# Turned source rows kept in SBUF replace one gather of 32 in the second stage of a graph network kernel

## What is computed

```python
h = relu(layernorm(x))
msg = relu(cat(h[src], h[dst], edge_attr) @ msg_W1 + b1) @ msg_W2 + b2
agg = segment_sum(msg, dst)
x = x + layer_norm(h + relu(cat(h, agg) @ upd_W1 + c1) @ upd_W2 + c2)      # layer 0
h = relu(layernorm(x))
x_l, x_r = h @ W_l.T + b_l, h @ W_r.T + b_r                                # 4 heads of 32
z = leaky_relu(x_l[src] + x_r[dst], 0.2)        # every node also has a loop to itself
alpha = softmax over the edges of a target of (z . att)
x = x + elu(segment_sum(alpha * x_l[src], dst) + bias)                     # layer 1
```

## Time and profile before

| | |
|---|---|
| median of 3 runs | 4952.78 us (4950.47 to 4958.61) |
| the profiled execution | 4911.11 us, span 4909.3 us |
| instructions | 83259 |
| busy share | PE 71%, PEld 56%, DVE 47%, ACT 43%, POOL 60% |
| mean granted TensorE clock | 0.784 of 2.4 GHz |
| indirect gathers | 1517 in stage one, 1553 in stage two |
| stage one, stage two | about 77 to 2445 us and 2472 to 4890 us |

### The profile page before, as it was taken

The page is one execution under the profiler, slowest core; times in us unless marked ns, Lnnn a source line. Parts: engine busy times, 40 slices in busy tenths (PEclk is TensorE's granted clock), DMA queues, the critical chain, the costliest instruction groups (busy, mean ns, idle before and its releaser), DMA issues.

```text
span 4909.3 us, 83259 instructions
## 1 busy us (share of the span) xinstructions
PE 3481.4 (71%) x21162; PEld 2765.1 (56%) x21162; DVE 2314.5 (47%) x11248; ACT 2101.0 (43%) x7367; POOL 2929.4 (60%) x3121
## 2 busy tenths in 40 slices
PE   4777777777776777776756777776767676777666
PEld 4666566565665666665635555555555555555555
DVE  3444444444444444444435455454555455545555
ACT  3344444444444444444434444444444444444444
POOL 6666666666656566665456656665566566666664
PEclk7677777777777767677778888888888888888888
DMA  5333343444343334333322222222222222222221
GB/s 151 111 112 112 110 113 109 113 113 112 111 113 109 111 111 113 111 112 110 87 74 71 69 67 71 71 71 69 69 70 70 67 70 70 70 71 71 70 71 49
DMA packets 345123, 444.82 MB, mean 91 GB/s; under 512 B 159013, under 2 KB 200835, under 8 KB 344639
## 3 DMA queue, kind: packets, MB, share of 16 engines
q1 hardware_dynamic: 245999, 238.05, 16.7%
q0 software_dynamic: 98240, 201.20, 16.0%
q10 hardware_dynamic: 400, 0.20, 0.0%
HBM read 419.07 MB, written 20.07 MB: 89 GB/s over the span
## 4 chain that ended last, share of the span: by engine, by line
issue 26%; DVE 22%; another core or an unknown queue 20%; PE 19%; ACT 11%; DVEq 2%; DMA 0%; ACTq 0%; SPq 0%
PE bank L2381 4%; PE bank L2387 3%; DVE t_logit L2507 3%; PE bank L1632 3%; DVE m_pre L1729 3%; DVE lone L905 2%; ACT t_z L2443 2%; PE bank L2402 2%; DVE t_zt L2500 2%; ACT t_a_row L2426 2%; ACT t_pen L2445 1%; ACT t_a_edge L2421 1%; PE bank L1620 1%; ACT lone L1688 1%
## 5 line engine op out<-in xcount | busy, mean ns | idle before, releaser
L970 POOL DMA_INDIRECT t_ring<-tab_l,src_t x1553 | 1465.3, 944 | 981.3 <-issue 406.3
L970 POOL DMA_INDIRECT m_ring<-tab_a,src_t x1517 | 1440.0, 949 | 949.5 <-issue 394.4
L2381 PE MATMUL bank<-t_ring,t_a_edge 128*128 128x128 f32 x3106 | 547.9, 330 | 686.8 <-ACT t_a_edge L2421 618.0
L1632 PE MATMUL bank<-w,m_attr_t 128*128 128x128 f32 x3128 | 817.5, 391 | 92.9 <-issue 80.1
L2381 PEld LDWEIGHTS bank<-t_ring,t_a_edge 128*128 128x128 f32 x3106 | 461.6, 228 | 739.7 <-ACT t_a_edge L2421 667.9
L1632 PEld LDWEIGHTS bank<-w,m_attr_t 128*128 128x128 f32 x3128 | 701.1, 275 | 172.9 <-issue 123.2
L2443 ACT ACTIVATE t_z<-bank 128x512 f32<-128x512 f32 x391 | 233.4, 597 | 1136.4 <-PE bank L2402 648.9
L1729 DVE TENSOR_TENSOR m_pre<-bank,m_ring 128x512 f32<-128x512 f32 (+1 forms) x391 | 263.9, 675 | 964.3 <-remote 668.1
L2500 DVE TENSOR_TENSOR t_zt<-bank,t_z 128x512 f32<-128x512 f32 x391 | 270.1, 691 | 890.0 <-issue 727.4
L1670 ACT ACTIVATE m_hid<-m_pre 128x512 f32<-128x512 f32 x391 | 246.4, 630 | 755.3 <-issue 430.3
L2387 PE MATMUL bank<-t_zt,att_wn 128*128 128x512 f32 x782 | 523.2, 760 | 2.9 <-DMA t_ring<-tab_l,src_t 2.9
(11 more groups left out here) (264 smaller groups left out, 5780.6 us busy)
## 6 DMA issues: line engine op xcount, KB each, us to landing
m_ring<-in_edge_attr_dram SPq DMA_DIRECT2D x390, 256.0 KB
t_rows<-dst_rows SPq DMA_DIRECT2D x196, 256.0 KB
m_rows<-dst_rows SPq DMA_DIRECT2D x196, 192.0 KB
t_ring<-tab_l,src_t POOLq DMA_INDIRECT x1553
m_ring<-tab_a,src_t POOLq DMA_INDIRECT x1517
lone<-tab_l SPq DMA_DIRECT2D x1408, 0.5 KB
m_win<-tab_b SPq DMA_DIRECT2D x391, 24.0 KB
t_win<-tab_r SPq DMA_DIRECT2D x391, 24.0 KB
```

What stands on the lines that cost most here:

```text
L970: pool.indirect_dma_start(out=r.got[u][0:rows, j, :], out_offset=None, in_=table, in_offset=bass.IndirectOffsetOnAxis(ap=k.src_t[0:rows, g ...
L1632: pe.matmul(p_hid[q % 2][:, e], lhsT=attr_t[q % 2][:, e], rhs=k.w1[:, 2, :], start=True, stop=False)
L2381: last = pe.matmul(p_nd[q % 2][:, 3 * W:3 * W + P], lhsT=a_edge[q % 2][:, j, :], rhs=column(k, r, g, j), start=(j == 0), stop=(j == J - 1))
```

## The change

In stage two the groups with g % 8 == 3 from 19 to 387 (`chosen`, 47 groups) no longer gather their fourth j. In stage one, once x of a node tile is final, SP stores it to a new table `tab_x`, and DVE later copies the turned x_l of that tile from `k.acc` over it in `k.X` (the last two tiles: at the start of stage two). In each of the eight slots ahead of a chosen group, DVE copies 7 columns and ACT 9 from `k.X` into `r.chosen`, at columns given by registers. PE transposes `r.chosen` into PSUM, ACT copies that to `r.chosen_rows`, and PE uses both in place of the gathered rows. SP fetches the ids of a chosen group (one DMA of 128 single ids per round) and, since `k.X` no longer holds x, one tile of `tab_x` per round for `tile_o`.

```diff
+def chosen(k, g):
+    return g % SPAN == 3 and 2 * SPAN <= g < k.groups - 1
+
+def choose_columns(nc, eng, k, r, s, g, first, many, move, done):
+    n, i = (g + SPAN - 2) // SPAN, (g - 2) % SPAN
+    if not many or not chosen(k, n * SPAN + 3):
+        return
+    if i == 0:
+        if n == 2:
+            eng.wait_ge(r.s_turned, 1)
+        eng.wait_ge(r.s_chosen_ids, 16 * (n - 1))
+        after(eng, s["t_zp"], (n - 2) * SPAN + 4 if n > 3 else 0)
+    first += i * CHOSEN
+    _, rows = nc.values_load_multi_w_load_instructions(
+        r.chosen_ids[n % 2][:, first:first + many], engines=[eng.engine], min_val=0, max_val=k.N - 1,
...
+    for q in range(many):
+        last = move(r.chosen[n % 2][:, first + q:first + q + 1], r.left[:, bass.ds(rows[q], 1)])
+    last.then_inc(done, 1)
...
-        for j in range(J - (lone(k, g) if table is k.tab_l else picked(k, g))):
+        for j in range(J - (lone(k, g) + chosen(k, g) if table is k.tab_l else picked(k, g))):
...
+            if u == 6 and c is not None:
+                hold(dve, s["n_zb"], c + 1)
+                hold(dve, s["n_xst"], 16 * (c + 1))
+                dve.tensor_copy(x_tile(c), k.acc[:, 0, cols(c)])
...
+        def sp_nodes(sp, b):
+            hold(sp, s["n_x"], b + 1)
+            sp.dma_start(k.tab_x[cols(b), :], x_tile(b)).then_inc(s["n_xst"], 16)
...
+        def loaded_nodes(dve, b):
+            if b < looped:
+                dve.wait_ge(r.s_x[b % 2], 16 * (b // 2 + 1))
+                return x_in[b % 2][:]
...
@@ stage two, fast_sync
+                    if u == 1 and rnd >= 3 and rnd - 3 < looped:
+                        sp_nodes(sp, rnd - 3)
+                    if g % SPAN == SPAN - 1 and g // SPAN >= 1:
+                        fetch_chosen(sp, k, r, t["src"], g // SPAN + 2)
@@ stage two, fast_tensor
+                        if chosen(k, g):
+                            pe.wait_ge(r.s_chosen_v, g - SPAN * 2 + SPAN - 3)
+                            pe.wait_ge(r.s_chosen_s, g - SPAN * 2 + SPAN - 3)
+                            turned = r.chosen[g // SPAN % 2][:]
+                            after(pe, s["t_o"], g // U - 2)
+                            pe.transpose(p_rows, turned, k.ident[:]).then_inc(r.s_turn, 1)
...
-                        for j in range(J):
+                        for j in range(J - chosen(k, g)):
...
+                        if chosen(k, g):
+                            last = pe.matmul(p_z[q % 2][:, (J - 1) * P:EG], lhsT=k.ident[:], rhs=turned,
+                                             start=False, stop=True)
@@ stage two, fast_scalar
+                        if chosen(k, g):
+                            act.wait_ge(r.s_turn, g // SPAN - 1)
+                            act.activation(r.chosen_rows[g // SPAN % 2][:], p_rows, ACT.Copy).then_inc(r.s_rows, 1)
...
+                    if not tail:
+                        choose_columns(nc, act, k, r, s, rnd * U + u, CHOSEN_BY_VECTOR, CHOSEN - CHOSEN_BY_VECTOR,
+                                       lambda out, col: act.activation(out, col, ACT.Copy), r.s_chosen_s)
@@ stage two, fast_vector
+                    if rnd == 0 and u == 2:
+                        dve.wait_ge(k.m["n_xst"], k.n_stored)
+                        dve.tensor_copy(r.left[:, both], k.acc[:, 0, both]).then_inc(r.s_turned, 1)
+                    if not tail:
+                        choose_columns(nc, dve, k, r, s, rnd * U + u, 0, CHOSEN_BY_VECTOR, dve.tensor_copy, r.s_chosen_v)
```

More of the change, by code:

```diff
@@ L35 @@
 SOONER = 2
+SPAN = 8
+CHOSEN = P // SPAN
+CHOSEN_BY_VECTOR = 7
 LEAD = 5
@@ L146, in gnn_program @@
         k.tab_l = dram("tab_l", [NP, P], F32)
+        k.tab_x = dram("tab_x", [NP, P], F32)
         k.tab_r = dram("tab_r", [NP, P], F32)
@@ L867, in landed @@
 def landed(k, g):
-    return 16 * sum(J - lone(k, a) for a in range(g % U, g + 1, U))
+    return 16 * sum(J - lone(k, a) - chosen(k, a) for a in range(g % U, g + 1, U))
 def lone_landed(r, g):
@@ L881, in column @@
         return r.lone[g // EVERY % 2]
+    if j == J - 1 and chosen(k, g):
+        return r.chosen_rows[g // SPAN % 2][:]
     return r.got[g % U][:, j, :]
@@ L906, in pick_columns, with fetch_chosen @@
     last.then_inc(done, 1)
+def chosen(k, g):
[12 more added lines that the diff above has]
+        r.chosen_ids[n % 2][:, first:first + many], engines=[eng.engine], min_val=0, max_val=k.N - 1,
+        skip_runtime_bounds_check_because="src names rows of the node features, as the gathers take it")
+    for q in range(many):
+        last = move(r.chosen[n % 2][:, first + q:first + q + 1], r.left[:, bass.ds(rows[q], 1)])
+    last.then_inc(done, 1)
+def fetch_chosen(sp, k, r, src, n):
+    g = n * SPAN + 3
+    if not chosen(k, g):
+        return
+    if n > 2:
+        after(sp, r.s_chosen_v, SPAN * (n - 3))
+        after(sp, r.s_chosen_s, SPAN * (n - 3))
+        sp.wait_ge(r.s_chosen_ids, 16 * (n - 2))
+    sp.dma_start(r.chosen_ids[n % 2].rearrange("o (p a) -> o p a", a=1),
+                 src[g * EG:(g + 1) * EG].rearrange("(o p j) -> o p j", o=1, j=J)[:, :, J - 1:J], allow_slow_non_contiguous=True
+                 ).then_inc(r.s_chosen_ids, 16)
 def fetch_picked(sp, k, m, src, n):
@@ L1225, in sp_pair @@
         def sp_pair(sp):
+            sp.wait_ge(s["n_x"], alone + 1)
+            sp.dma_start(k.tab_x[both, :].rearrange("(t p) d -> p t d", p=P), pair_x).then_inc(s["n_xst"], 16)
             sp.wait_ge(s["n_rows"], alone + 1)
@@ L1566, in fast_sync @@
             sp.sem_clear(range(min(nums), max(nums) + 1))
+            for b in range(NR - 3, alone):
+                sp_nodes(sp, b)
             for b in range(NR - 4, alone):
@@ L2056, in edges_attention @@
         r.s_lone, r.s_ids = [sems.one(f"t_lone{q}") for q in range(2)], sems.one("t_ids")
-        s = k.both
+        r.s_turned, r.s_chosen_ids, r.s_chosen_v, r.s_chosen_s, r.s_turn, r.s_rows, r.s_x_end = (
+            sems.one("t_" + n) for n in ("left", "ch_ids", "ch_v", "ch_s", "ch_turn", "ch_rows", "x_end"))
+        r.s_x = [sems.one(f"t_x_in{q}") for q in range(2)]
+        r.chosen_ids = [w[0:1, :].bitcast(I32) for w in (k.w2, k.u2)]
+        r.left = k.X[:].rearrange("p t d -> p (t d)")
+        s = dict(k.both, t_x=sems.one("t_x"), t_s=sems.one("t_s"), t_cd=sems.one("t_cd"))
         s_end = k.late["t_end"]
@@ L2089, in edges_attention @@
         end_o = [tile_o] + ring("end_o", len(rest) - 1, [P, P])
+        r.chosen, r.chosen_rows = ring("chosen", 2, [P, P]), ring("chosen_rows", 2, [P, P])
+        x_in = ring("x_in", 2, [P, P])
+        x_end = k.HT[:, k.NP:k.NP + len(rest) * P]
+        both = slice((k.tiles - 2) * P, k.tiles * P)
+        p_rows = p_out[:, 0:P]
         tiny = sb("tiny", [P, 1])
@@ L2131, in pe_turn, with own_nodes, sp_nodes, dve_o @@
             pe.transpose(p_out[:, 0:P], tile_el[:], k.ident[:]).then_inc(s["t_tp"], 1)
-        def dve_o(dve, b, o):
+        def own_nodes(b):
+            return k.X[:, bass.ds(b, 1), :].rearrange("p a d -> p (a d)")
+        def loaded_nodes(dve, b):
+            if b < looped:
+                dve.wait_ge(r.s_x[b % 2], 16 * (b // 2 + 1))
+                return x_in[b % 2][:]
+            dve.wait_ge(r.s_x_end, 16)
+            return x_end[:, (b - looped) * P:(b - looped + 1) * P]
+        def sp_nodes(sp, b):
+            if b == 0:
+                sp.wait_ge(k.m["n_xst"], k.n_stored)
+                sp.dma_start(x_end.rearrange("p (t d) -> p t d", d=P),
+                             k.tab_x[looped * P:k.tiles * P, :].rearrange("(t p) d -> p t d", p=P)).then_inc(r.s_x_end, 16)
+            after(sp, s["t_o"], b - 1)
+            sp.dma_start(x_in[b % 2][:], k.tab_x[b * P:(b + 1) * P, :]).then_inc(r.s_x[b % 2], 16)
+        def dve_o(dve, b, o, nodes):
             hold(dve, s["t_tp"], b + 1)
@@ L2323, in step @@
                 dve_elu(dve, b)
-                dve_o(dve, b, tile_o)
+                dve_o(dve, b, tile_o, own_nodes(b))
             each_tile(dve, step)
```

21 lines of the change are left out of this document (13 added, 8 removed).

## The result

| | before | after |
|---|---|---|
| median of 7 runs | 4951.37 us (4950.47 to 4969.27) | 5002.43 us (4986.14 to 5014.38) |
| ratio | | 1.0091, 95% interval 1.0073 to 1.0108 |
| profiled execution | 4911.11 us, span 4909.3 | 5007.41 us, span 5005.6 |
| busy share | PE 71, PEld 56, DVE 47, ACT 43, POOL 60% | PE 70, PEld 55, DVE 53, ACT 49, POOL 58% |

The account below looks back on a forecast made before the run. Stage two was taken as bounded by a circle of engines waiting for each other; −23.5 + 7 + 2 + 2.5 = −12 us on the median of 4953 gave 4941 us, own range 4920 to 4955, eight in ten 4903 to 4985.

Parts of the forecast that it names:

- What bounds stage two: Stage two: engines waiting for each other set a 6.20 us period; 147 `t_z` releases were "remote", against 221 by PE.
- 47 gathers, −23.5: Stage two: each gather left out saves 0.50 us over four slots, −23.5 us in all, ends 0 and −59.
- PE's part +7: PE on chosen groups: added transpose and plain float32 matmul cost 14 to 24 us, partly hidden; +7, ends 0 and +24.
- Stage one, +2.5: Stage one: 47 DVE copies of 128x128, 10.4 us, a quarter counted; +2.5 us, ends 0 and +10.
- SP, 0: SP in stage two: one `tab_x` load and one fetch of 128 ids per round, needed many slots later; 0.
- The port, +2: Stage two: column copies slow POOL's gathers by some 5 ns each, 7.5 us; +2 taken, ends 0 and +8.
- The columns, 0: 376 slots of stage two: loads and copies, 1.3 us on DVE and 1.5 on ACT, covered by idle time; 0.
- the forecast's own case: Whole kernel: the terms' sum holds, median 4941 us, own range 4920 to 4955, chance 0.42.
- The fourth case: Between `own_x` and `t_zt`: DVE's copies come late in two slots a round, +38 us, 4979; chance 0.20.
- The case of the whole pitch: Stage two: each missing gather saves its full 1.25 us, −59 in all, 4906 us; chance 0.15.

Follow-up runs that it names:

- second trace of before: The kernel before, unchanged, run again for a second profile: 4951.92 us.
- runs at 0.895: Change with 8 and 8 columns: registers loaded once in eight slots, register columns on DVE alone, on ACT alone: 3882.53, 3878.06, 3880.58 us; kernel before 3938.46.
- the gathers alone: The change without column copies, register loads or id fetches, the 47 gathers still left out: 4920.68 us, ratio 0.9934 to the kernel before.
- 8 and 8: The change with DVE and ACT copying 8 columns each in place of 7 and 9: 4961.07 against 4947.93 us before, ratio 1.0028.
- first trace of before: The first profile of the unchanged kernel, the one the prediction read: profiled execution 4911.11 us.
- 4 and 12: The change with DVE copying 4 columns and ACT 12: 4953.07 against 4949.55 us before, ratio 1.0004; run again 4951.39, ratio 1.0007.
- the ladder: The change with its eight slots splitting 16 ids differently between DVE and ACT, to time each load's length: one run, 4983.41 us.

## Why the prediction was wrong

- **What bounds stage two** (a circle; a late signal, looked for at POOL, in 147 slots): the circle holds, the reading of the late signal does not. In the code `t_z` waits for one signal, `t_zp`, which PE raises with its last transpose. The forecast took PE's end at 3521.18 as true and laid the 1.65 us to something that comes 2.1 us after the fourth gather. In the second trace of before, the stretch from the first weighted sum to the signal is 4.33 us in slots where PE's record ends within half a us of the signal and the mean granted clock is 0.63 of 2.4 GHz. It is 4.32 in late slots, where the records show 0.98 (PE's end by the record: 4.20 and 2.68). In the runs at 0.895 the lateness is gone and PE's records end with the signal, after 2.9 us. That PE was slow in both kinds of slots, and the page's modelled ends wrong in one, fits all this; it was not shown by itself.
- **47 gathers, −23.5, with PE's part +7:** undersized, −16.5 against −33 measured with both (and stage one's part) in. How the difference divides between the two terms was not measured.
- **Stage one, +2.5; SP, 0:** right within the noise, −1 us measured (−7 to +2).
- **The port, +2:** nothing seen. Gathers take 944 ns with 7 copies beside and 943 with 8, and their pitch stays 1.25. The trace does not agree with the Trainium skill's rule ("SBUF — State Buffer", section "SBUF: two separate sides", on float32 copies that lock out GpSimd) for copies of one column; longer copies were not tried.
- **The columns, 0: the step that failed.** It read "a register load 0.60 and 0.55", then "DVE: 0.60 + 7 × 0.10 = 1.3 us", "ACT: 0.55 + 9 × 0.109 = 1.5 us", "Both are covered in ordinary slots: 0". Measured, the columns cost 72 to 84 us over the gathers alone. Two things were wrong in it.
  - The prices were those of loads of 8 ids, and the change loads 7 and 9 from the first and the eighth. With the measured 1.04 and 1.97, and the copies' 0.84 and 0.98 from start to end, DVE needs 2.0 us and ACT 3.1, of which some 0.4 lie beside its earlier work. That leaves 1.6 and 2.7 us to be covered. Against the idle times in the rows (2.28 on average and 1.26 behind the short slot on DVE; 2.64 to 3.15 and 1.57 in the short slot on ACT), both are short in and behind the short slots, and ACT has nothing to spare in the others. Mending the loads (8 and 8) won 25 to 40 us.
  - "Covered" does not hold even at its own price: with 8 and 8, whose loads take 0.60 and 0.55, the columns still cost 46 us. About 10 of them are DVE's lateness behind the short slots; what takes the rest stays open. The rows gave one short slot and an average, and the average hides the spread: in the first trace of before, 41 of 360 `t_zt` had under 1.27 us of idle time ahead of them.
- **The range of the forecast's own case** (4920 to 4955 "from the ends of its terms") is narrower than those ends, which add up to 4894 to 4997. The time lies above even these. The chances add up as 0.40, 0.27 and 0.33, not 0.41, 0.27 and 0.32.
- **The fourth case** (DVE late, 4979) named the mechanism and one place of it, the slot of `tile_o`, but priced it at 38 us on one engine. It was DVE and ACT, and the columns took 72 to 84 us. No row showed a load of 7 or 9 ids, so its price was unknown and had an upper end above 0.60 that the range left out.
- **The case of the whole pitch** is what three versions of the change, with 8 and 8, showed at the higher clock: −56 to −60.

## What to carry to other kernels

Price an instruction by one of the same shape; a register load of 9 values from an odd place is not one of 8 with one added. In this kernel it paid to load registers from SBUF in fours, from a start that is a multiple of four (0.06 us an id in place of 0.22), and to load a few too many rather than start elsewhere. When two covered pieces of work go behind the same idle time, add them, and compare the sum with the spread of the idle time and its shortest slots, not with the average, for each engine by itself. Mending one of two late engines can win as much as mending both: here it did.

## What the runs showed of the hardware

- Register loads from SBUF, from a start on a multiple of four: about 0.1 us, and 0.25 for four ids or 0.23 for one, by the ladder; a load on ACT from another start costs 0.22 us for each id (9 ids 1.97, 14 ids 3.05). DVE was not measured from such a start.
- A DVE copy of one column took 0.072 us by busy time at a fixed column and 0.121 at a register's in stage two, 0.099 in stage one.
- The same kernel ran in 4950 and in 3938 us with mean granted clocks of 0.78 and 0.895, and the same saving was worth 33 us in one (by its closest version) and 56 to 60 in the other. At the lower clock PE's stretch is the longest part of a slot (4.3 of 6.2 us); at the higher one POOL's gathers set the pace (3.85 a slot by 1.25 us are the period of 4.82).
- Open: what takes the last 30 us with 4 and 12 columns at the usual clock, and what the change itself does at the higher clock, at which it was not run. One rival for the first was not tested: the register loads and operations lengthen the instruction lists, and on the pages the instruction queue q14 moved 3.41 MB in the change and 2.55 before.
